# Graph attention layer: x.T kept in the place of V.Wh, one more pair transposed ahead, small products for the last s, first x asked for on two queues

## The reference

```python
Wh = x @ W.T                       # 8192 x 256
s_i, s_j = Wh @ r[:256, 0], Wh @ r[256:, 0]
e = s_i[:, None] + s_j[None, :]    # 8192 x 8192
e = where(e >= 0, e, 0.2 * e)
e = where(adj == 0, -inf, e)
attention = softmax(e, axis=1)
out = layernorm(x + gelu(attention @ Wh))
```

## Time and profile before

| | us |
|---|---|
| median of 3 timed runs | 1565.75 |
| lowest and highest | 1565.62, 1567.47 |
| profiled execution, its own time | 1564.46 |
| span of its trace | 1562.7 |
| mean granted TensorE clock | 0.993 |

### The profile page before, as it was taken

How to read it: one execution, slowest core, us unless ns; L and a number is a source line. 1 busy time by engine, 2 the same in 40 slices (tenths; PEclk the granted TensorE clock), 3 DMA queues, 4 the chain that set the end, 5 groups by cost and what they waited for, 6 DMA issues and landing times.

```text
span 1562.7 us, 37391 instructions
## 1 busy us (share of the span) xinstructions
PE 1544.4 (99%) x12849; PEld 1539.1 (98%) x12849; DVE 1484.0 (95%) x1854; ACT 1210.7 (77%) x1608; POOL 461.0 (29%) x667
## 2 busy tenths in 40 slices
PE   9999999999999999999999999999999999999996
PEld 9999999999999999999999999999999999999996
DVE  6799999999999999999999999999999999999996
ACT  6788887877787777787787777878778777777774
POOL 1112223333323333322333332233332233323222
PEclk9999999999999999999999999999999999999998
DMA  9746777869589686858877776877778687787861
GB/s 205 126 63 85 105 100 108 113 82 132 73 120 119 101 111 91 120 75 126 114 107 100 102 114 80 128 103 104 109 101 117 84 128 95 99 121 92 115 89 42
DMA packets 295102, 163.99 MB, mean 105 GB/s; under 512 B 12320, under 2 KB 291104, under 8 KB 295072
## 3 DMA queue, kind: packets, MB, share of 16 engines
q0 software_dynamic: 278976, 142.12, 69.6%
q1 hardware_dynamic: 16096, 21.54, 5.1%
HBM read 289.41 MB, written 8.42 MB: 191 GB/s over the span
## 4 chain that ended last, share of the span: by engine, by line
PE 95%; issue 3%; ACT 1%; POOL 1%; DVE 0%; DMA 0%; SPq 0%; POOLq 0%; ACTq 0%; DVEq 0%
PE acc L798 30%; PE acc L788 30%; PE acc L791 30%; PE acc L716 1%; PE acc L723 1%; PE acc L718 1%; PE acc L701 1%; ACT P_hi L468 0%; DMA Pw<-in_x 0%; PE acc L743 0%; ACT gates L369 0%; PE acc L747 0%; PE acc L745 0%; POOL fits L331 0%; POOL adj_in L265 0%
## 5 line engine op out<-in xcount | busy, mean ns | idle before, releaser
L788 PE MATMUL acc<-WV_hi,P_hi 128*128 (+1 forms) x4096 | 998.3, 282 | 3.1 <-ACT P_hi L468 2.5
L791 PE MATMUL acc<-WV_lo,P_hi 128*128 (+1 forms) x4096 | 996.9, 281 | 0.0
L788 PEld LDWEIGHTS acc<-WV_hi,P_hi 128*128 128x128 f32 x4096 | 773.8, 189 | 5.1 <-ACT P_hi L468 3.0
L791 PEld LDWEIGHTS acc<-WV_lo,P_hi 128*128 128x128 f32 x4096 | 771.7, 188 | 0.0
L468 ACT CAST P_hi<-Pw 128x1024 fp32r<-128x1024 f32 x512 | 535.7, 1046 | 288.5 <-DVE Pw L594 153.0
L594 DVE SCALAR_TENSOR_TENSOR Pw<-R_row,X,gatesT 128x512 f32<-128x512 f32 x1024 | 710.4, 746 | 0.5 <-issue 0.5
L604 DVE TENSOR_TENSOR P_lo<-Pw,P_hi 128x1024 fp32r<-128x1024 f32 x512 | 624.7, 1220 | 41.5 <-ACT P_hi L468 35.0
L265 POOL DMA_DIRECT2D adj_in<-in_adj x512 | 330.6, 653 | 884.6 <-ACT gates L369 856.0
L798 PE MATMUL acc<-WV_hi,P_lo 128*128 (+1 forms) x4096 | 575.4, 283 | 0.0
L369 ACT ACTIVATE gates<-adj_in 128x1024 uint8<-128x1024 bf16 x512 | 536.8, 1049 | 27.9 <-DMA adj_in<-in_adj 27.9
L798 PEld LDWEIGHTS acc<-WV_hi,P_lo 128*128 128x128 f32 x4096 | 526.6, 189 | 0.0
(11 more groups left out here) (95 smaller groups left out, 365.4 us busy)
## 6 DMA issues: line engine op xcount, KB each, us to landing
adj_in<-in_adj POOLq DMA_DIRECT2D x512, 256.0 KB, 5.5
out<-y SPq DMA_DIRECT2D x64, 128.0 KB, 6.1
y<-in_x POOLq DMA_DIRECT2D x60, 128.0 KB, 6.0
Pw<-in_x SPq DMA_DIRECT2D x48, 128.0 KB, 4.9
R_row<-w_rows SPq DMA_DIRECT2D x15, 256.0 KB, 6.8
x_res<-in_x SPq DMA_DIRECT2D x20, 128.0 KB, 4.2
w_in<-in_L_gnn_W SPq DMA_DIRECT2D x1, 256.0 KB, 2.8
w_rows<-w_in SPq DMA_DIRECT2D x1, 32.0 KB, 2.1
```

The source lines that it names most:

```text
L788: nc.tensor.matmul(acc[r_][:, v, 0:HC], P_hi[:, u % 2, par, bass.ts(v, P)], WV_hi[:, k, :], start=(first and u == 0 and par == 0), stop=False)
L791: nc.tensor.matmul(acc[r_][:, v, 0:FOUT], P_hi[:, u % 2, par, bass.ts(v, P)], WV_lo[:, k, :], start=False, stop=False)
```

## The change

It has these parts.

- `xT_hi[j]` and `xT_lo[j]` lie in the first 512 columns of the two blocks of `WV_hi` and `WV_lo` where V.Wh of the same pair is written later, so each pair has a place of its own. Transposes, their copy and the remainder run one pair further ahead from pair 8 on (`x_behind`); TensorE waits before transposes j for the remainder of pair j - 2.
- Behind pair 2, ScalarE and VectorE copy the columns of W.r, high and low, side by side into a new tile `wr`. The last two pairs' s takes eight products for each pair: high x by the four columns of `wr`, and low x by two; VectorE adds the two halves (two instructions in place of one copy).
- r and half of the first block of x are asked for on ScalarE's queue instead of SP's.
- TensorE runs three products on zeros at the start in place of four. It makes the W.r product before the first transposes of x, and in a pair the four products with low W stand behind the four with high W; the wait for low W stands between them.
- ScalarE waits for the last Wh product behind its first copy to `P_hi`, not ahead of it; one copy of V is moved into the second stage; the size sums of V.Wh are spread otherwise over the first two row blocks.

```diff
-        xT_hi = P_hi[:, 1]
-        xT_hi_read = P_hi[:].bitcast(F32)[:, 1]
-        xT_lo = P_hi[:, 0]
+        WV_hi_read = WV_hi[:].bitcast(F32)
+        xT_hi = [WV_hi[:, 2 * j:2 * j + 2, :].rearrange("p k c -> p (k c)")[:, 0:BANK] for j in range(NC // 2)]
+        xT_hi_read = [WV_hi_read[:, 2 * j:2 * j + 2, :].rearrange("p k c -> p (k c)")[:, 0:BANK] for j in range(NC // 2)]
+        xT_lo = [WV_lo[:, 2 * j:2 * j + 2, :].rearrange("p k c -> p (k c)") for j in range(NC // 2)]
...
-        ps_s = [acc[0][:, j, 0:4] for j in range(2)]
+        ps_s = [acc[0][:, j, 0:8].rearrange("p (r c) -> p r c", c=4) for j in range(2)]
...
+        def x_behind(j):
+
+            if j == 8:
+                return [10, 11]
+            return [j + 2] if j < 8 else [j + 3] if j + 3 < NC // 2 else []
...
-            sp.dma_start(r_in[:], r.rearrange("(u p) a -> p (u a)", p=P),
-                         allow_slow_non_contiguous=True).then_inc(s_r, 16)
             for n in range(NC // 4):
                 if n >= 4:
 
                     sp.wait_ge(s_xT, 2 * (n - 4) + 2)
-                for a in range(4):
+                for a in range(2 if n == 0 else 4):
                     sp.dma_start(x_in[n % 4][32 * a:32 * a + 32].rearrange("p s f -> p (s f)"),
                                  x_m[n, a]).then_inc(s_x[n % 4], 16)
...
+            act.dma_start(r_in[:], r.rearrange("(u p) a -> p (u a)", p=P),
+                          allow_slow_non_contiguous=True).then_inc(s_r, 16)
+            for a in range(2, 4):
+                act.dma_start(x_in[0][32 * a:32 * a + 32].rearrange("p s f -> p (s f)"), x_m[0, a]).then_inc(s_x[0], 16)
...
-            copy_x(0)
             act.wait_ge(s_wr, 1)
             nc.scalar.copy(w_hi[:, :, FOUT:HC],
                            acc[1][:, 3, 0:2 * KT].rearrange("p (k c) -> p k c", c=2)).then_inc(s_wTc, 1)
+            copy_x(0)
             copy_x(1)
             for j in range(NP - 2):
-                if j < NP - 3:
-                    high_part(j)
-                    copy_x(j + 2)
-                else:
-                    copy_x(NP - 1)
-                    high_part(j)
+                high_part(j)
+                for m in x_behind(j):
+                    copy_x(m)
+                if j == 2:
+                    act.wait_ge(s_wTc, KT + 1)
+                    nc.scalar.copy(wr[:, :, 0:2], w_hi_read[:, :, FOUT:HC]).then_inc(s_wrc, 1)
...
-            nc.scalar.copy(WV_hi[:, NC - 4:NC, FOUT], V[:, NC - 4:NC]).then_inc(s_vh, 1)
...
-                            if not before and c == 0 and u == 0:
-                                act.wait_ge(s_wh, NP)
                             nc.scalar.copy(P_hi[:, u % 2], Pw[u][:]).then_inc(s_hi, 1)
                             if not before and c == 0 and u < 2:
+                                if u == 0:
+                                    act.wait_ge(s_wh, NP)
                                 late_high_part(NC - 2 + u)
+                            if not before and c == 0 and u == 2:
+                                act.wait_ge(s_hi0, NC)
+                                nc.scalar.copy(WV_hi[:, NC - 4:NC, FOUT], V[:, NC - 4:NC]).then_inc(s_vh, 1)
                             if before and c in steps:
                                 steps[c](t - 1, 1 - r_, u)
-                            if sizes_from is not None and (c > 0 if before is False else c % 2 == 0):
-                                n = sizes_from + (4 * c + u - 4 if before is False else 2 * c + u)
-                                if n < NC // 2 and (before or n < 20):
-                                    wh_size(n)
+                            if not before and c > 0 and u > 0:
+                                wh_size(3 * c + u - 4)
+                            if second and c in (2, 4, 6) and 2 * c + u < 15:
+                                wh_size(17 + 2 * c + u)
...
-                nc.vector.tensor_copy(S[:, 2 * j:2 * j + 2, :], ps_s[j % 2].rearrange("p (r c) -> p r c", c=2)).then_inc(s_s, 1)
+                nc.vector.tensor_copy(s_low[:], ps_s[j % 2][:, :, 2:4]).then_inc(s_sl, 1)
+                dve.wait_ge(s_sl, j - (NP - 2) + 1)
+                nc.vector.tensor_tensor(S[:, 2 * j:2 * j + 2, :], ps_s[j % 2][:, :, 0:2], s_low[:], ALU.add).then_inc(s_s, 1)
...
-                x_low(j + 2)
+                for m in x_behind(j):
+                    x_low(m)
+                if j == 2:
+                    dve.wait_ge(s_wl, KT + 1)
+                    nc.vector.tensor_copy(wr[:, :, 2:4], P_lo[:].bitcast(F32)[:, 1, :, FOUT:HC]).then_inc(s_wrc, 1)
                 if j == 18:
                     transpose_piece(0, 0)
-            x_low(NP - 1)
...
-            for _ in range(4):
+            for _ in range(3):
                 nc.tensor.matmul(acc[1][:, 3, 0:2 * P], zeros[:, 0:P], zeros, start=True, stop=True)
...
+                if j >= 2:
+                    pe.wait_ge(s_xTl, j - 1)
...
-                    pe.wait_ge(s_wl, KT + 1)
                 if j >= 3:
 
                     pe.wait_ge(s_s, j - 2)
                 for r_ in range(2):
                     for k in range(KT):
-                        nc.tensor.matmul(ps_wh[j % 3][:, r_, :], xT_hi[:, j % 2, bass.ts(KT * r_ + k, P)],
+                        nc.tensor.matmul(ps_wh[j % 3][:, r_, :], xT_hi[j][:, bass.ts(KT * r_ + k, P)],
                                          w_hi[:, k, :], start=(k == 0), stop=False)
-                        nc.tensor.matmul(ps_wh[j % 3][:, r_, :], xT_hi[:, j % 2, bass.ts(KT * r_ + k, P)],
+                if j == 0:
+                    pe.wait_ge(s_wl, KT + 1)
+                for r_ in range(2):
+                    for k in range(KT):
+                        nc.tensor.matmul(ps_wh[j % 3][:, r_, :], xT_hi[j][:, bass.ts(KT * r_ + k, P)],
                                          w_lo[:, k, :], start=False, stop=False)
...
-            transpose_x(0)
...
+            transpose_x(0)
             transpose_x(1)
             for j in range(NP - 2):
                 wh_product(j)
-                transpose_x(j + 2)
-
-            def three_products(target, j, r_, columns):
-
+                for m in x_behind(j):
+                    transpose_x(m)
+
+            def s_product(j):
+
+                pe.wait_ge(s_xTl, j + 1)
+                pe.wait_ge(s_wrc, 2)
+                for r_ in range(2):
+                    for k in range(KT):
+                        nc.tensor.matmul(ps_s[j % 2][:, r_, :], xT_hi[j][:, bass.ts(KT * r_ + k, P)], wr[:, k, :],
+                                         start=(k == 0), stop=False)
+                        last = nc.tensor.matmul(ps_s[j % 2][:, r_, 0:2], xT_lo[j][:, bass.ts(KT * r_ + k, P)],
+                                                wr[:, k, 0:2], start=False, stop=(k == KT - 1))
+                last.then_inc(s_s2, 1)
...
```

34 lines of the change are left out of this document (16 added, 18 removed).

## The result

The changed kernel takes 1562.77 us (median of 20 runs, 1560.37 to 1566.46) against 1566.03 us of the kernel before (20 runs, 1563.0 to 1570.9) on the same chip: ratio 0.9979, with a 95% interval of 0.997 to 0.9988. It is faster by 0.2%, or 3.3 us. Measured a second time it took 1563.7 us against 1565.91, ratio 0.9982 (0.9972 to 0.9991), or 2.2 us between the medians. So "2 to 3 us" is as near as these runs come.

A forecast was written before the change was run, and what follows sets the result against it. TensorE was taken to bound the kernel, with gains possible only in the first 79 us. Start 1.8, small products 0.6 and end clock 1.4 sum to 3.8 us; 1565.75 less that gives 1562.0 us, range 1559.9 to 1565.2.

The forecast's parts named there:

- faster by over 0.2%: Whole kernel: a time under 1562.6 us, given a chance of 0.58.
- The loop: Loop over pairs, first stage: same products and transposes in another order, TensorE without a gap, so gain 0.
- The order at the start: Start: W.r product, copy and remainder ahead of x's transposes; transpose to first Wh product 1.37 us, not 2.23; gain 0.86.
- The arrival of x: Start: the first x asked for earlier by using ScalarE's queue; gain 0.35 us, between 0 and 1.5.
- The clock at the start: Start: the stretch at half speed may not come, as TensorE waits less; gain 0.6 us, from 0 to 1.7.
- the first rise may be later: Start: the opposite case, full clock coming later because one product on zeros is gone; no separate size given.
- The small products: End of the first stage: fewer small products, so line 793's product (was 766) starts earlier; gain 0.6 us.
- The clock at the end: End of the first stage: low stretch of half the length, 3.4 us in place of 6.9; gain 1.4 us.
- the step's upper bound: End of the first stage: at most 2.7 us from a better clock, limited by the wait for `Pw`.
- The second stage: Second stage: products unchanged, moved size sums and a small copy fit ScalarE's idle time; cost 0.
- The transfer rival: Pair loop: x and adj share DMA engines, ScalarE waits for adj, some 2 us lost; 1564.9 us, chance 0.11.
- the start's terms: Start: gains of 0.86 from order, 0.35 from x's arrival and 0.6 from the clock, together 1.8 us.

The follow-up runs named there:

- one_ahead: Changed kernel with transposes, copy and remainder one pair ahead to the end, as in the kernel before: 1566.13 us, ratio 0.9998.
- four_zeros: Changed kernel with four products on zeros at the start in place of three: 1562.92 us, ratio 0.9976.
- before_wr_first: Kernel before, with the W.r product, its copy and its remainder ahead of those of the first x: 1564.89 us, ratio 0.9996.
- after_again: The changed kernel itself, unaltered, measured and traced a second time: 1563.70 us, ratio 0.9982.
- all_on_sp: Changed kernel with r and all of x asked for on SP's queue again, in the old order: 1562.39 us, ratio 0.9976.
- sp_four_zeros: Changed kernel with r and all of x on SP's queue again and four products on zeros: 1561.58 us, ratio 0.9971.
- sp_four_between: Changed kernel with r and x on SP's queue, four zeros products, and six late products ahead of line 793's product: 1562.53 us, ratio 0.9982.
- late_between: Changed kernel with the first six late products ahead of line 793's product instead of behind it: 1563.09 us, ratio 0.998.

## Why the prediction was right, and where it wasn't

The time was right: 1562.0 predicted, 1562.77 and 1563.7 measured, both in the range. Whether it is the forecast's "faster by over 0.2%" the two ratios leave open, 0.9979 on one side of that line and 0.9982 on the other. Its terms were not all right, and errors cancelled, so part of the hit is luck.

- **The loop, 0.** Right: 1.895 us for a pair before and after.
- **The order at the start, 0.86.** The mechanism was right, 1.37 us from transpose to product predicted and 1.33 measured where the clock is full. In the changed kernel it is 1.77, because the clock is low: 0.46 gained.
- **The arrival of x, 0.35.** Wrong. This step took W's arrival as given and asked only about x. x did not come earlier (7.04 against 6.75), and W came 1.58 us later, because r was asked for on the second queue. In the changed kernel W is the last thing waited for. That takes both, W late and the clock low: where W was as late and the clock full (`one_ahead`, `four_zeros`), TensorE waited for x again, at 7.15 and 6.91.
- **The clock at the start, 0.6.** Wrong in sign in both traces. The step named the case ("the first rise may be later") and chose the other side. Full clock comes at 13.56 us only; weight loads of 333 ns mark the stretch from 6.07 on. The rows of the kernel before could not have settled it either: kernels with the same start have the low clock there or not (1.71 and 0.95 us for the W.r products). Together the start was to gain 1.8 us and lost 0.87 at pair 1 (0.76 at the first small product).
- **The small products, 0.6.** Right: 2.11 us in place of 2.82 in the trace, 0.71.
- **The clock at the end, 1.4.** The size was right in this trace: 7.55 - 6.01 = 1.54 us, with a low stretch of half the length, as chosen. The reason was not: the step gave the shorter small products and the missing wait for pair 31 as what halves the stretch. `before_wr_first` has neither, and takes 5.99 us with a clock of 0.79. `after_again`, `all_on_sp`, `four_zeros` and `sp_four_zeros` have the changed kernel's work there, and their windows from 70 to 78 us show 0.79, 0.63, 1.00 and 1.00. So the largest single term was right by luck, as far as the runs show. (Without any low clock the stretch takes 4.65 us, 2.9 less than before; the step's upper bound was 2.7.)
- **The second stage, 0.** Right that the size sums are free: TensorE waits 1.2 us for `P_hi` between 80 and 340 us in both kernels. Not right that nothing there moves: the late adj load at 345 us costs 1.0 to 1.1 us in both traces of the changed kernel. The moved size sums are not shown to be its cause, since `before_wr_first` has such a wait without them.
- **The rivals.** The transfer rival did not show in the changed kernel, and did in `four_zeros` and `sp_four_between`, with 2.06 and 1.69 us on TensorE against the "some 2" predicted. Had the start's terms held, this rival would have taken them.

In the profiled executions the sum is +0.76 - 0.71 - 1.54 = -1.49 us up to the second stage and +1.45 in it: 0 in all (1564.46 to 1564.42). The medians differ by 3.3 and 2.2. Part of this is that the profile of before was a lucky one: its rest of 1485.4 us is the shortest of the fourteen in the table, whose median is 1486.75. With that, before comes to 79.08 + 1486.75 = 1565.8, its measured median, but the changed kernel to 77.59 + 1486.75 = 1564.3, 0.6 to 1.6 above. The prediction had taken the distance between profile and median as the same for both kernels; it isn't. What fills the remaining 0.6 to 1.6 us is open. An end without a low stretch in many of the timed executions would do it, as the second stage's start at 75.65 in `four_zeros` shows. Timed executions have no trace, but their mean granted clocks speak rather against this: it is 0.996 in the profiled execution of the changed kernel and in 12 more of its 20, and 0.997 in one, while `four_zeros` and `sp_four_zeros`, whose ends have no low clock, have 0.997 in their profiled ones. As the start's low clock is missing from some traces, this is a hint and no more.

Which part of the change pays is settled only roughly. The parts put into the kernel before one by one move its median by at most 1.6 us, which no comparison here resolves. Taken out of the changed kernel, one part stands out: without the further pair of transposes (`one_ahead`) the ratio is 0.9998 (0.9986 to 1.001), against 0.9978 and 0.998 of the two kernels beside it, and in the trace 0.8 us of that is ScalarE's order behind pair 29. The prediction gave running further ahead no gain in the loop, and the trace of `one_ahead` agrees (12.59 to 65.55, or 1.891 us for a pair); what the prediction took from it at the end stood inside the clock term. The DMA part gains nothing (1.0008 alone; 0.9976 for the kernel without it).

## What to carry to other kernels

Keep a DMA of many tiny pieces behind the transfer that everything waits for: on the same queue behind W, r let it land at 3.75 to 4.02 us, on a second queue, asked for within 0.1 us of W, it made W land at 5.01 to 5.51. Before a start-up gain is counted, look for the next transfer that is timed against it: here a start 1.4 us earlier turned into a 2 us wait twenty microseconds later, because x and adj share the engines. When two kernels differ by 0.2%, compare stretches and not spans, and say of each profile where it lies among its own timed runs. And before a shorter stretch of low clock is credited to a change, look at a trace in which that stretch's work is unchanged.

## What was not expected of the hardware

- 512 packets of 4 bytes on one queue delayed 256 KB on another by 1.0 to 1.8 us (W at 5.01 to 5.51 us against 3.75 to 4.02), though they hold 2 KB. In the first 0.8 us of transfers 217 of them went and 14 packets of W.
- The clock at the start does not follow from the instructions. With three products on zeros and over 1 us idle TensorE was at 1.2 GHz until 13.56 us in the changed kernel, and made the W.r products at 2.4 GHz in `one_ahead`; with four and no idle time it was at 1.2 GHz there in `sp_four_zeros` and at 2.4 in `sp_four_between`. What decides between them is open.
- The same instructions at the end of the first stage ran wholly at 2.4 GHz (4.65 us from line 793's product to the copy, in `four_zeros` and `sp_four_zeros`), or with part of it at 1.2 GHz (6.01, and 7.38 in `all_on_sp`, with a mean clock of 0.79 and 0.63 from 70 to 78 us). In `late_between` the low clock came 1.4 us after the second stage had started, amid full-width products without a gap, behind a wait of 1.8 us. What decides is open here too.
